# The mixed rows of the last convolution: all four sets on VectorE instead of two on VectorE and two on GpSimd

## The reference

```
# layer 0
x0 = depthwise_conv7x7(x) + bias; layer norm over channels
logits = x0 @ Wg; top 2 of 8 experts per pixel, softmax weights, capacity limit
moe = sum over the 2 experts of gate * (gelu(x0 @ W1[e]) @ W2[e])
y = x + x0 + layer_scale * moe
# layer 1, on y (coordinate attention, then a 3x3 convolution)
h, w = mean of y over rows, mean of y over columns
a_h, a_w = sigmoid(Wh @ hswish(bn(W1 @ h))), sigmoid(Ww @ hswish(bn(W1 @ w)))
out = silu(bn(conv3x3(y * a_h * a_w)))
```

## Time and profile before

| | |
|---|---|
| time, median of 3 runs | 5306.66 us (5299.35 to 5312.86) |
| profiled execution | 5302.44 us, of which the span of the trace 5300.7 |
| busy in the span | PE 4498.9, DVE 2826.9, POOL 2563.1, ACT 1545.8 us |
| output stage | 3540 us to the end |
| L1422, POOL's gathers | 784, 1195 ns each in the mean |

### The profile page before, as it was taken

One profiled execution on the slowest core, in us unless ns is written; L12 is line 12 of the kernel. 1 busy time (PEld: TensorE's weight loads), 2 busy tenths in 40 slices (PEclk: granted clock), 3 DMA queues, 4 the chain that ended last, 5 costly groups with the idle time before them and its releaser, 6 DMA issues. The chain is left out here.

```text
span 5300.7 us, 67784 instructions
## 1 busy us (share of the span) xinstructions
PE 4498.9 (85%) x19429; PEld 2513.6 (47%) x19429; DVE 2826.9 (53%) x5000; ACT 1545.8 (29%) x3715; POOL 2563.1 (48%) x2316
## 2 busy tenths in 40 slices
PE   8999998942259999999999999975787778777778
PEld 3555565941124444444444444443444444444444
DVE  0002221789943333333333333338988898888896
ACT  2223333736023333333333333321111111111111
POOL 0000000030378888888888100027778777777772
PEclk9999999965679999999999999987888888888888
DMA  8887776960255555555555322244445444454441
GB/s 168 185 178 194 196 196 159 281 190 0 68 155 167 173 170 167 171 172 169 167 170 171 84 69 68 68 138 155 149 138 172 158 142 141 149 174 143 140 139 56
DMA packets 1012557, 788.78 MB, mean 149 GB/s; under 512 B 591313, under 2 KB 904578, under 8 KB 1008258
## 3 DMA queue, kind: packets, MB, share of 16 engines
q1 hardware_dynamic: 724786, 354.36, 26.6%
q0 software_dynamic: 84224, 258.61, 15.5%
q10 hardware_dynamic: 203344, 173.40, 10.2%
HBM read 445.38 MB, written 340.66 MB: 148 GB/s over the span
## 5 line engine op out<-in xcount | busy, mean ns | idle before, releaser
L1174 ACT ACTIVATE hid<-hid_ps,b_cols 128x512 f32<-128x512 f32 (+1 forms) x1056 | 707.9, 681 | 1320.4 <-PE hid_ps L1124 986.8
L1422 POOL DMA_INDIRECT y_ring<-xy,index_o x784 | 936.8, 1195 | 225.1 <-issue 217.8
L1124 PE MATMUL hid_ps<-xt,w_sb 128*128 128x512 f32 (+1 forms) x2112 | 939.6, 588 | 1.6 <-issue 0.8
L1134 PE MATMUL y_ps<-hid,w_sb 128*128 128x512 f32 (+1 forms) x2112 | 936.5, 586 | 0.4 <-DVE yt L1204 0.4
L457 POOL DMA_INDIRECT xy<-twice,slots x784 | 785.0, 1001 | 255.1 <-issue 254.5
L1471 PE MATMUL mp<-mix,taps_o 128*128 128x392 f32 x1536 | 620.7, 556 | 0.0
L1471 PE MATMUL mp<-mix,mixed_o 128*128 128x392 f32 x1536 | 588.3, 533 | 13.1 <-issue 7.9
L1204 DVE TENSOR_SCALAR yt<-y_ps,b_cols,scale_col 128x512 f32<-128x512 f32 (+1 forms) x264 | 211.7, 802 | 679.3 <-PE y_ps L1134 483.2
L1124 PEld LDWEIGHTS hid_ps<-xt,w_sb 128*128 128x128 f32 x2112 | 381.9, 191 | 372.9 <-issue 369.7
L373 PE MATMUL cv<-xin,toep 56*56 56x448 f32 x5376 | 543.5, 542 | 15.8 <-ACT rows L318 9.5
L1134 PEld LDWEIGHTS y_ps<-hid,w_sb 128*128 128x128 f32 x2112 | 380.8, 190 | 369.2 <-issue 367.3
(11 more groups left out here) (311 smaller groups left out, 4928.4 us busy)
## 6 DMA issues: line engine op xcount, KB each, us to landing
rows_in<-xy SPq DMA_DIRECT2D x1040, 64.5 KB
xy<-rows_out ACTq DMA_DIRECT2D x1040, 64.0 KB
xin<-in_x_dram SPq DMA_DIRECT2D x256, 196.0 KB
conv<-rows ACTq DMA_DIRECT2D x256, 196.0 KB
pix<-conv SPq DMA_DIRECT2D x224, 224.0 KB, 4.9
xn<-hat SPq DMA_DIRECT2D x112, 448.0 KB, 4.4
chunk<-xn POOLq DMA_DIRECT2D x112, 448.0 KB
logits<-xn SPq DMA_DIRECT2D x112, 448.0 KB
```

Of the source, the lines that this page charges most:

```text
L1124: pe.matmul(hid_ps[f][:, 0:cols], w1_sb[e][:, f * 128:(f + 1) * 128], xt[e % 2][:, 0:cols], start=True, stop=True).then_inc(hid_done, 1)
L1134: last = pe.matmul(y_ps[:, 0:cols], w2_sb[e][:, f, :], hid[e % 2][:, f, 0:cols], start=(f == 0), stop=(f == NH - 1))
L1174: act.activation(hid[e % 2][:, f, 0:cols], hid_ps[f][:, 0:cols], ACT.Gelu, bias=b1_cols[:, e * NH + f:e * NH + f + 1]).then_inc(hid_ready, 1)
L1422: pool.indirect_dma_start(out=y[ch][:, j, :, :].rearrange("p h c -> p (h c)"), out_offset=None, in_=xy[:, :], in_offset=bass.IndirectOffse ...
```

## The change

`mix_outer` is gone from POOL's program. Its four operations stand behind L1676 in `attend` on DVE, and the last of them signals one semaphore, `mixed`, which takes the place of `mixed_dve` and `mixed_pool` in PE's wait and in SP's. The table of mixed weights, which had the name `mixed`, is now `mid_taps`; it is the same table.

```diff
@@ sync
-                    sp.wait_ge(mixed_dve, g * 2)
-                    sp.wait_ge(mixed_pool, g * 2)
+                    sp.wait_ge(mixed, g * 2)
@@ gpsimd
-            def mix_outer(n):
-
-                img, b = n % 2, n // 2 % 2
-                even, odd = even_odd(summed[b][:, img * HW:(img + 1) * HW])
-                if n == 0:
-                    pool.wait_ge(margins_set, 1)
-                pool.wait_ge(scaled, n + 1)
-                if n >= 2:
-                    pool.wait_ge(part_done, (n - 1) * PARTS)
-                last = ROW_PAIRS - 1
-                pool.tensor_scalar(mix[img][:, 0, 0, 1:1 + W], odd[:, 0, :], -1.0, None, ALU.mult)
-                pool.tensor_copy(mix[img][:, 3, last, 1:1 + W], even[:, last, :])
-                pool.tensor_tensor(mix[img][:, 0, 1:, 1:1 + W], odd[:, 0:last, :], odd[:, 1:, :], ALU.subtract)
-                pool.tensor_tensor(mix[img][:, 3, 0:last, 1:1 + W], even[:, 0:last, :], even[:, 1:, :], ALU.subtract
-                                   ).then_inc(mixed_pool, 1)
...
                     gather(g * NCHK + ch)
-                    if g and ch in (0, 3):
-                        mix_outer(g * 2 - 2 + (ch == 3))
-            mix_outer(N - 2)
-            mix_outer(N - 1)
@@ tensor
                 if at == OLD:
-                    pe.wait_ge(mixed_dve, n + 1)
-                    pe.wait_ge(mixed_pool, n + 1)
+                    pe.wait_ge(mixed, n + 1)
@@ vector, end of attend
-                dve.tensor_tensor(mix[img][:, 2, :, 1:1 + W], odd, even, ALU.subtract).then_inc(mixed_dve, 1)
+                dve.tensor_tensor(mix[img][:, 2, :, 1:1 + W], odd, even, ALU.subtract)
+                last = ROW_PAIRS - 1
+                dve.tensor_scalar(mix[img][:, 0, 0, 1:1 + W], odd[:, 0, :], -1.0, None, ALU.mult)
+                dve.tensor_copy(mix[img][:, 3, last, 1:1 + W], even[:, last, :])
+                dve.tensor_tensor(mix[img][:, 0, 1:, 1:1 + W], odd[:, 0:last, :], odd[:, 1:, :], ALU.subtract)
+                dve.tensor_tensor(mix[img][:, 3, 0:last, 1:1 + W], even[:, 0:last, :], even[:, 1:, :], ALU.subtract
+                                  ).then_inc(mixed, 1)
```

More of the change, by code:

```diff
@@ L1265, in output_phase @@
         taps = sb("taps_o", [C, 3, 3 * C])
-        mixed = sb("mixed_o", [C, 2, 3 * C])
+        mid_taps = sb("mid_taps", [C, 2, 3 * C])
         w1_rows, w1_t = sb("w1_rows", [RED, C]), sb("w1_t", [C, RED])
@@ L1309, in output_phase @@
         half_scaled, scaled = sem("half_scaled"), sem("scaled")
-        mixed_dve, mixed_pool = sem("mixed_dve"), sem("mixed_pool")
+        mixed = sem("mixed_rows")
         part_done, copied, joined, silu_done = sem("part_done"), sem("copied_o"), sem("joined"), sem("silu_done")
@@ L1468, in part @@
                 buf = img if o < GROUPS // 2 else 1 - img
-                weights = (taps[:, 0], mixed[:, 0], mixed[:, 1], taps[:, 2])[kind]
+                weights = (taps[:, 0], mid_taps[:, 0], mid_taps[:, 1], taps[:, 2])[kind]
                 for kw in range(3):
@@ L1579, in _ @@
             do(dve.tensor_copy(ww_t[:], cpre[3][0:RED, 256:384]))
[L1580 to L1583, removed]
+            do(dve.tensor_tensor(mid_taps[:, 0], taps[:, 0], taps[:, 2], ALU.add))
+            do(dve.tensor_tensor(mid_taps[:, 1], mid_taps[:, 0], taps[:, 1], ALU.subtract))
+            do(dve.tensor_tensor(mid_taps[:, 0], mid_taps[:, 0], taps[:, 1], ALU.add))
+            do(dve.tensor_scalar(mid_taps[:], mid_taps[:], 0.5, None, ALU.mult))
             dve.wait_ge(const_in, 17 * 16)
```

## The result

The changed kernel takes 5376.65 us (median of 4 runs, 5367.14 to 5398.9) against 5304.18 before: 1.0142 times, 95% interval 1.0123 to 1.016, some 75 us slower. 5390 was forecast, with 5340 to 5415 as the range. Its profiled execution took 5372.7, the span is 70.2 us longer than before.

What follows compares the result with a forecast made beforehand. No engine is full over the span; in the output stage VectorE (89% busy) sets the end, where PE has run dry. Rows 112, stalls -53 and clock 27 gave +86 us: 5390 forecast, range 5340 to 5415.

Steps and rivals of the forecast that it cites:

- Rows: Four operations per image added to DVE ahead of PE's transposes: 3.6 us each image, 31 images, +112 us in all.
- Stalls: DVE additions held up by POOL's row operations: 99 us removed, only part on the path, -44 over 14 pairs.
- rival 1: Output stage: stalls wholly on the path, DVE the bound everywhere, no clock term; +13 us, 5318; chance 8%.
- Clock: PE's longer idle stretches lower its granted clock: 1.75 us a pair, +27 us over 15.5 pairs (0 to 42).
- a low clock of over 4 us: Sign: behind PE's idle before the transposes, the low clock lasts over 4 us in most cases.
- the 102.6 us of a pair without stalls: Output stage: quick pair's 103.13 us less 0.5 still won, 3.1 us under the mean pair.
- The ends: Outside the 14 pairs: the last one's stalled additions and one usual stall, 4.6 us on the path, -9 together.
- a wait that I had put down at nothing: PE's wait for POOL's semaphore, 1.78 us in the trace: its removal was to win nothing.
- TensorE as the pace: Rival: DVE's added 3.6 us hidden behind queued matmuls while stalls go; -53 us, 5252; chance 4%.
- the edge rows: Rival: two 56-element rows on DVE each held up by a POOL gather, up to 1.2 us; +74, 5464; chance 4%.
- the gathers: Rival: DVE's stalls stay, as POOL's gathers and not its row arithmetic cause them; 5442; chance 4%.
- pairs alike: Sign: all pairs of images in the output stage take about 111.5 us, without the alternation.

Runs made afterwards that it cites:

- r1: Changed kernel with the rows of kinds 0 and 3 left out for all images but the first two: 0.9956 times the kernel before, 5269.5 us.
- r2: Changed kernel with the four row operations made twice, one behind the other: 1.0431 times the kernel before, 5521.1 us.
- r4: Changed kernel with the rows moved behind the next chunk's add and sums, except the last image's: 0.9903 times the kernel before, 5244.9 us.
- r6: Kernel before, with PE repeating the next part's matmuls twice in its idle stretch behind each image's rows: 0.9986 times the kernel before, 5298.9 us.
- r11: r4 with two PE repeats in the idle stretch and two more ahead of the wait for pooled sums: 0.9805 times the kernel before, 5193.6 us.
- r7: Changed kernel plus two POOL subtractions of 1120 elements at the old place, on tiles nobody else uses: 1.0301 times the kernel before, 5466.6 us.
- r8: As r7, but with two POOL fills of the same 1120 elements, which read nothing: 1.0221 times the kernel before, 5428.5 us.

## Why the prediction was right

The time and the main mechanism were right: the rows cost their full length where PE had run dry, and the stalls had cost only a part of theirs. That the sum came out so near is in part luck, as two of its terms missed in opposite directions. By its own steps, over the 14 pairs first (101 - 44 + 24 = 81 forecast, 75.1 us measured):

- **Rows, 28 x 3.6 = 101 us.** Right: 3.49 us of work. r1 and r2 show that all of it counts, and r4 that it is for its place.
- **Stalls, -44.** The right size for a typical pair, and 11 too much for the sum: r1 gives -32.9, as it has late releases of its own (57.9 and 60.3 us among its first images) and one slower early pair (106.0 us). That a quick and a slow pair lay beside each other in one trace (5.2 us for 8.3 of stall) was the reading on which the forecast stood; it puts 63% on the path, and r1 37%. Rows less stalls would have given +13 and rival 1.
- **Clock, 14 x 1.75 = +24.** Mis-sized as a term: the changed kernel less r1 is 107.9 us, of which 97.7 is work, so about 10 were left for the longer idle stretch, 14 less than forecast. The sign named for it, a low clock of over 4 us behind most of the stretches, failed: it was so in 11 of 28 images, where it had been in 15 of 28 before. A longer idle stretch did not bring a longer low clock behind it. In its place the clock has a larger part that the steps did not see. Keeping it up gains 74 us after the change and 7 before. The low clock behind the idle stretches was there already (0.87), but what it cost went into the stalls' place: with it kept up DVE's stalls grew by nearly what its idle time lost (r6); without stalls it shows. I had taken the 102.6 us of a pair without stalls as the floor, and it held the clock's cost: r11 makes all the rows and has pairs of 98.8 us.
- **The ends.** From the last of the 14 pairs' marks to the end of the span: before 5300.7 - 5145.72 = 155.0 us, after 5370.9 - 5222.58 = 148.3; -6.7 where -9 + 3.6 = -5.4 was forecast. At the start, from the stage's first addition to the first mark, +2.5 (108.0 to 110.5) for two images' rows of 3.5 each: PE had waited 5.12 us for POOL's first rows, a wait that I had put down at nothing.
- Sum: 75.1 + 2.5 - 6.7, and 0.7 less ahead of the stage, is the 70.2 us of the span. The forecast had 86, 16 too many: some 6 in the pairs (14 too much of clock and 3 of rows, less the 11 of the stalls), 5 at the start, 3 for the clock outside the pairs, and 2 at the end and ahead of the stage.

Of the rivals, TensorE as the pace is out by its 9.71 us of idleness; the edge rows last 0.18 us; the gathers hold nothing up (L1584 1085 ns). What I said of pairs alike was wrong for second images, some 51.6 or 53.9 us, and PE's idle stretch was 9 to 9.75 us in 19 of 28 images where 8 to 9 was said.

## What to carry to other kernels

Price moved work by where it lands: on an engine that another one waits for with an empty queue, each microsecond counts, and a few instructions later it can be free (r4 against the changed kernel, 2.4% for one move). A stall found in a trace is worth its length only where its engine would not have waited next: 37% of it here in the kernel before (r1), 85% at a place where PE waits (r7). Neighbouring periods with and without it tell the direction (5.2 us for 8.3), but two of them are few for the size. And before work is moved off GpSimd for its stalls, see what then becomes visible: here a low TensorE clock whose cost did not show while the stalls were there.

## What the runs showed of the hardware beside that

Two POOL subtractions of 2.9 us hold a 1.09 us addition up, to 3.97 us at most, and two fills of 1.0 us don't (r7, r8). It goes the other way too: in the changed kernel a gather of POOL takes 1.00 us beside DVE's reductions and joins, and up to 3.99 beside its two-input scaling of an image (L1648). PE's signals can reach DVE, ACT and POOL 2 to 5 us after its records end, in the first image of a pair only, in 13 of 14 pairs of r8, two of the changed kernel and none of r4; the cause is open. Repeating matmuls whose results are thrown away raised the granted clock of the stage from 0.84 to 0.93 and took 1.4% off the time.
